# The gated mixture of half 0: summed by TensorE in two PSUM banks and evicted by ScalarE, and the norm of its tiles 0 to 3 applied by ScalarE

## The reference, cut to what matters

```python
x = x + jnp.tanh(g_xattn[0]) * wkv(w, u, _layernorm(x), ctx_2048)      # stage 0 makes y, stage 1 starts from this x
x = x + jnp.tanh(g_ffn[0])   * ternary_ffn(_layernorm(x), w_gate_up, w_proj)
x = x + jnp.tanh(g_xattn[1]) * masked_attention(_layernorm(x), ctx_2048, mask)
x = x + jnp.tanh(g_ffn[1])   * fp8_linear(_layernorm(x), weight, weight_scale, bias)
```

## Time and profile before

| | |
|---|---|
| median of 3 runs | 140.72 us (139.71 to 140.81) |
| the profiled execution | 141.18 us, of which the span from first to last instruction is 139.4 us |
| PE busy | 119.2 us (86% of the span) |
| DVE busy | 116.5 us (84%) |
| ACT busy | 85.5 us (61%) |
| POOL busy | 32.7 us (23%) |
| chain that ended last, by engine | PE 47%, DVE 32%, issue 7%, ACT 6%, DMA 3%, POOL 2% |
| mean granted TensorE clock | 0.951 |

### The profile page before, as it was taken

One profiled execution on the slowest core, in us unless ns is written; L12 is line 12 of the kernel. 1 busy time (PEld: TensorE's weight loads), 2 busy tenths in 40 slices (PEclk: granted clock), 3 DMA queues, 4 the chain that ended last, 5 costly groups with the idle time before them and its releaser, 6 DMA issues.

```text
span 139.4 us, 2211 instructions
## 1 busy us (share of the span) xinstructions
PE 119.2 (86%) x733; PEld 79.6 (57%) x743; DVE 116.5 (84%) x278; ACT 85.5 (61%) x163; POOL 32.7 (23%) x75
## 2 busy tenths in 40 slices
PE   5899788862899899999987999999996779496992
PEld 5799673420522346477653667777675657274581
DVE  5896999997993969999987897769997789995880
ACT  3197898028584777685765777856654534522962
POOL 7913000005000000000233802059334624401000
PEclk9999999995555999999999999999999999999999
DMA  4999950000000000000000000000000000000026
GB/s 132 288 353 350 388 131 2 0 0 0 0 0 0 0 5 2 0 0 0 0 5 0 2 0 0 5 0 0 0 2 5 0 0 0 2 0 0 2 97 208
DMA packets 7110, 6.90 MB, mean 50 GB/s; under 512 B 1336, under 2 KB 6842, under 8 KB 7098
## 3 DMA queue, kind: packets, MB, share of 16 engines
q1 hardware_dynamic: 7088, 6.75, 15.1%
q10 hardware_dynamic: 10, 0.00, 0.0%
HBM read 5.70 MB, written 1.05 MB: 48 GB/s over the span
## 4 chain that ended last, share of the span: by engine, by line
PE 47%; DVE 32%; issue 7%; ACT 6%; DMA 3%; POOL 2%; ACTq 1%; POOLq 0%; DVEq 0%
PE ps L848 8%; PE ps L849 7%; PE ps L907 5%; DVE xs L1214 4%; DVE stats L1125 4%; PE ps L1101 4%; PE ps L881 4%; DVE sums L1156 3%; PE ps L770 3%; PE ps L768 3%; DMA gate_row<-_L_ffn_weight_scale_dram 3%; DVE xn L1137 3%; PE ps L813 2%; PE ps L994 2%; DVE hbuf L1294 2%
## 5 line engine op out<-in xcount | busy, mean ns | idle before, releaser
L848 PE MATMUL ps<-wT,xhi 128*128 128x512 bf16 x60 | 23.8, 396 | 1.3 <-ACT xlo L545 1.0
L849 PE MATMUL ps<-wT,xlo 128*128 128x512 bf16 x60 | 23.5, 392 | 0.2
L907 PE MATMUL ps<-wT,wgu_raw 128*128 128x256 bf16 x128 | 16.6, 273 | 0.1
L418 POOL TENSOR_SCALAR ve<-mv 128x2 f32<-128x2 f32 (+2 forms) x12 | 2.3, 192 | 59.4 <-DVE mv L1131 59.3
L907 PEld LDWEIGHTS ps<-wT,wgu_raw 128*128 128x128 f16 x128 | 12.4, 98 | 1.6 <-DVE wgu_raw L1281 0.3
L1125 DVE BATCH_NORM_STATS2 stats<-xs 128x6 f32<-128x256 f32 x32 | 12.3, 414 | 1.1 <-DMA xs<-in_x_dram 0.7
L586 ACT ACTIVATE wgu_raw<-ps 128x512 f16<-128x512 f32 x16 | 9.6, 597 | 5.5 <-PE ps L881 5.0
L534 ACT ACTIVATE wscale<-ps 128x1024 bf16<-128x1024 f32 x6 | 6.1, 1023 | 10.3 <-PE ps L770 10.3
L1137 DVE TENSOR_SCALAR xn<-xs,mv,rstd 128x256 f32<-128x256 f32 x26 | 9.5, 409 | 2.9 <-POOL rstd L419 2.1
L1294 DVE SCALAR_TENSOR_TENSOR hbuf<-ps,pscale,sil 128x512 f32<-128x512 f32 x11 | 8.2, 749 | 3.3 <-PE ps L849 3.3
L848 PEld LDWEIGHTS ps<-wT,xhi 128*128 128x128 f16 x64 | 6.4, 100 | 7.7 <-ACT xlo L545 1.5
(11 more groups left out here) (173 smaller groups left out, 281.9 us busy)
## 6 DMA issues: line engine op xcount, KB each, us to landing
wgu_raw<-in_L_ffn_w_gate_up_dram SPq DMA_DIRECT2D x4, 512.0 KB, 9.0
ctx_sb<-in_ctx_dram SPq DMA_DIRECT2D x2, 512.0 KB, 7.3
wp_raw<-in_L_ffn_w_proj_dram SPq DMA_DIRECT2D x1, 1024.0 KB, 10.2
out_dram<-xs SPq DMA_DIRECT2D x3, 256.0 KB, 2.2
xs<-in_x_dram SPq DMA_DIRECT2D x2, 256.0 KB, 2.9
xs<-in_x_dram SPq DMA_DIRECT2D x1, 512.0 KB, 6.7
wlin_raw<-in_L_ffn_weight_dram SPq DMA_DIRECT2D x1, 256.0 KB, 9.1
out_dram<-xs SPq DMA_DIRECT2D x2, 128.0 KB, 2.0
```

What stands on the lines that cost most here:

```text
L848: pe.matmul(ps[:, bank, :], xhi[:, h, c, o:o + P], w, start=(c == 0), stop=False)
L849: mm = pe.matmul(ps[:, bank, :], xlo[:, h, c, o:o + P], w, start=False, stop=(c == CH - 1))
L907: mm = pe.matmul(proj_at(i), part[:, n % 2, j * P:(j + 1) * P], wT[:, GU_PAIRS + f, j * C:(j + 1) * C], start=(first and f == 0 and j == 0 ...
```

## The change

TensorE now forms the sum x + tanh(g) * y itself. Two banks are used, 0 for tiles 0 and 1, and 1 for tiles 2 and 3. `mix_x` puts x there, by one float32 matmul of 256 columns per tile against the identity, in the place where the six dummies stood. `mix_y` then accumulates y onto it, in the place of `y_back(0)`: eight float32 matmuls of 128 columns, each with a block of y as the stationary operand and the identity scaled by tanh(g) (`ident_tg`, which ScalarE makes once near the start) as the moving one. ScalarE evicts the two banks to `res` (`mix_in`), ahead of `rest_in(0)`. VectorE's `mix_out` is gone; `mix_stats` is the old `ln_stats` with waits for the evictions. The norm of tiles 2 and 3 moves from VectorE to ScalarE, which now does all four in two steps. `invert(2)` moves on ScalarE from before the norm to behind `xn_low(1)`. `ffn_in(0)` and `ffn_in(1)` wait for one norm step each. `gate(0)` waits for the evictions and the statistics. The rest of the diff adapts counts.

```diff
@@ scalar
             act.preload_act_table_set("natural_log_exp_and_others")
+            act.wait_ge(ident_ready, 1)
+            act.wait_ge(tg_ready, 1)
+            act.activation(ident_tg[:, :], ident[:, :], ACT.Copy, scale=tg[:, 0:1]).then_inc(ident_tg_ready, 1)
             act.wait_ge(cols_ready, 2)
...
+            def mix_in(b):
+                act.wait_ge(mix_ps, b + 1)
+                act.activation(res[:, 2 * b:2 * b + 2, :].rearrange("p i c -> p (i c)"), ps[:, b, :], ACT.Copy).then_inc(mix_ready, 1)
...
             invert(1)
+            mix_in(0)
+            mix_in(1)
             rest_in(0)
             rest_in(1)
-            invert(2)
-            ln_apply(1, 0, TPC // 2, 1)
+            act.wait_ge(mix_ready, 2)
+            ln_apply(1, 0, 2, 1)
+            ln_apply(1, 2, 2, 1)
             xn_high(0)
             xn_high(1)
             xn_low(0)
             xn_low(1)
+            invert(2)
             invert(3)
@@ tensor
+            def mix_x():
+                pe.wait_ge(in_x[0], 16)
+                pe.wait_ge(in_x[1], 16)
+                pe.wait_ge(G_ready, CHUNKS * CH)
+                for i in range(TPC):
+                    o = (i % 2) * C
+                    pe.matmul(ps[:, i // 2, o:o + C], ident[:, :], xs[:, i, :], start=(i % 2 == 0), stop=False,
+                              skip_group_check=True)
+
+            def mix_y():
+                pe.wait_ge(y_ready, CH)
+                pe.wait_ge(ident_tg_ready, 1)
+                for i in range(TPC):
+                    for c in range(CH):
+                        o = (i % 2) * C + c * P
+                        mm = pe.matmul(ps[:, i // 2, o:o + P], y[:, c, i * P:(i + 1) * P], ident_tg[:, :], start=False,
+                                       stop=(i % 2 == 1 and c == CH - 1), skip_group_check=True)
+                    if i % 2:
+                        mm.then_inc(mix_ps, 1)
...
             def ffn_in(k):
...
-                pe.wait_ge(res_ready[1], (1, 1, 2, 3)[k])
-                if k == 0:
-                    pe.wait_ge(xn_ready_act, 1)
+                if k < 2:
+                    pe.wait_ge(ctxT_ready, CHUNKS * CH)
+                    pe.wait_ge(xn_ready_act, k + 1)
...
             def gate(n):
                 if n == 0:
-                    pe.wait_ge(G_ready, CHUNKS * CH)
+                    pe.wait_ge(mix_ready, 2)
+                    pe.wait_ge(mv_ready[1], 1)
...
-            keep_warm(WARM_FRONT, 0, wabs)
+            mix_x()
             for p in range(PAIRS):
                 weight_sums(p)
-            y_back(0)
+            mix_y()
@@ vector
-            def mix_out():
-                dve.wait_ge(tg_ready, 1)
-                dve.wait_ge(yT_ready, 2)
-                residual(1, 0, TPC, lambda i: ps[:, XN_BANKS[0][i // 2], (i % 2) * C:(i % 2 + 1) * C], lambda i: tg[:, 0:1], 1)
+            def mix_stats():
+                last = None
+                for i in range(TPC):
+                    if i % 2 == 0:
+                        dve.wait_ge(mix_ready, i // 2 + 1)
+                    now = step(dve.bn_stats(stats[:, i, :], res[:, i, :]))
+                    if i > 0:
+                        after(last)
+                        step(dve.bn_aggr(mv[:, 1, i - 1, :], stats[:, i - 1, :]))
+                    last = now
+                after(last)
+                dve.bn_aggr(mv[:, 1, TPC - 1, :], stats[:, TPC - 1, :]).then_inc(mv_ready[1], 1)
...
-            mix_out()
-            ln_stats(1, 0, TPC)
+            mix_stats()
             den_bonus(2)
             greatest_scales()
-            ln_apply(1, TPC // 2, TPC // 2, 1)
             den_scan(3)
```

More of the change, by code:

```diff
@@ L100, in gated_blocks @@
         neg_bf = sb("neg_bf", [P, P], BF16)
+        ident_tg = sb("ident_tg", [P, P])
         scales = sb("scales", [SCALE_ROWS, 512], BF16)
@@ L213, in gated_blocks @@
         tg_ready = sem("tg_ready")
+        ident_tg_ready = sem("ident_tg_ready")
+        mix_ps = sem("mix_ps")
+        mix_ready = sem("mix_ready")
         guard_rows = sem("guard_rows")
@@ L787, in y_back @@
                 pe.wait_ge(y_ready, CH * (h + 1))
[L789 to L793, removed]
+                pe.wait_ge(rest_ready, PAIRS)
+                pe.wait_ge(wl_f, 1)
                 for i in range(TPC):
@@ L804, in ffn_in @@
                 bank = XN_BANKS[k // 2][k % 2]
-                pe.wait_ge(res_ready[1], (1, 1, 2, 3)[k])
-                if k == 0:
-                    pe.wait_ge(xn_ready_act, 1)
-                else:
-                    pe.wait_ge(xn_ready[1], k)
+                if k < 2:
+                    pe.wait_ge(ctxT_ready, CHUNKS * CH)
+                    pe.wait_ge(xn_ready_act, k + 1)
+                else:
+                    pe.wait_ge(res_ready[1], k - 1)
+                    pe.wait_ge(xn_ready[1], k - 1)
                 for c in range(CH):
@@ L832, in channel_major @@
                 elif q < 2:
-                    pe.wait_ge(xn_ready_act, q + 2)
+                    pe.wait_ge(xn_ready_act, q + 3)
                 else:
@@ L1218, in residual @@
                 dve.wait_ge(res_ready[stage], count)
-            def mix_out():
-                dve.wait_ge(tg_ready, 1)
-                dve.wait_ge(yT_ready, 2)
-                residual(1, 0, TPC, lambda i: ps[:, XN_BANKS[0][i // 2], (i % 2) * C:(i % 2 + 1) * C], lambda i: tg[:, 0:1], 1)
+            def mix_stats():
[10 more added lines that the diff above has]
+                dve.bn_aggr(mv[:, 1, TPC - 1, :], stats[:, TPC - 1, :]).then_inc(mv_ready[1], 1)
             def mix_pair(k):
-                dve.wait_ge(yT_ready, k + 1)
-                residual(1, 2 * k, 2, lambda i: ps[:, XN_BANKS[1][k - 2], i * C:(i + 1) * C], lambda i: tg[:, 0:1], k)
+                dve.wait_ge(yT_ready, k - 1)
+                residual(1, 2 * k, 2, lambda i: ps[:, XN_BANKS[1][k - 2], i * C:(i + 1) * C], lambda i: tg[:, 0:1], k - 1)
             def weights_abs(p):
@@ L1347, in greatest @@
                 if q < 2:
-                    dve.wait_ge(xn_ready_act, q + 2)
+                    dve.wait_ge(xn_ready_act, q + 3)
                 else:
```

## The result

The changed kernel is slower. Median 142.57 us (141.45 to 144.45, four executions) against 140.22 (139.70 to 140.81) of before, 1.017 times. The ratios given from here on leave disturbed executions out (here that of 144.45 us, in e11 one of 177, whose trace is not read): 1.0127, 95% interval 1.0065 to 1.0190. That is clear of noise, though less than 2%, and the median lies outside the forecast range of 139.0 to 141.7. Timed again in experiment e11 the ratio is 1.0181 (1.0115 to 1.0246). The profiled execution took 141.45, its span is 139.6 us; it is the shortest of its kernel, so its trace shows the least of the loss.

What follows compares the result with a forecast made beforehand. It took the front as bound by VectorE's scan and the scales, then TensorE and ScalarE alternating, then ScalarE alone. Terms -1.05 + 0.55 - 0.1 = -0.6 us, against 140.72 giving 140.1; range 139.0 to 141.7.

Steps and rivals of the forecast that it cites:

- "the same": Whole kernel: no change its measurement can tell, neither under 139.3 us nor over 142.1; chance 0.69.
- The step that failed: GpSimd in the front: statistics 1.6 us sooner, shift at 31.7 instead of 33.31, its 1.2 us of lead unused.
- the front's -1.05: End of the front: ScalarE's norm starts at 32.9 instead of 34.05, so TensorE's turning and `xn_low(1)` come 1.05 us earlier.
- The moved inversion: ScalarE before the table load: a second invert of 1.28 us there gives back 0.55 of the 1.05 us gained.
- The clock: TensorE's clock over `weight_rest(3)`: returning from half earlier than 44.94, it adds 0.1 us of gain, `gate(1)` 0.6 sooner.
- the forecast -0.6: Whole kernel: sum of the terms -1.05, +0.55 and -0.1 us against the profiled execution of before.
- the base: Starting time for the sum: profiled execution 141.18 us, 0.46 above the median; the forecast was set against 140.72.
- `ident_tg` (0.40 us): Start of ScalarE: making the scaled identity takes 0.35 us, hidden in 0.54 us of idle time, so costs 0.
- the evictions: ScalarE ahead of `rest_in(0)`: two at 0.60 us, hidden in 5.45 us of idle time; `rest_in(0)` stays at 29.26.
- the statistics: VectorE in the front: without `mix_out`'s 1.64 us they start at 27.6 instead of 29.20, 1.6 us sooner.
- F: ScalarE behind the table load: an unseen stall up to 0.78 us puts `silu(0)` at 42.6, total 140.9; chance 0.02.
- C: TensorE's clock falls before 27.9 instead of 31.3, slowing `weight_rest(0)` and (1): +0.85 us, 141.6; chance 0.14.

Runs made afterwards that it cites:

- e11: The changed kernel, unedited, timed again beside the kernel before: ratio 1.0181 (1.0115 to 1.0246).
- e2: The changed kernel with one more wait: VectorE starts `den_scan(3)` only once GpSimd has written the shift; ratio to before 1.0017, median 140.35 us.
- e4: The kernel before with only the norm of all four tiles on ScalarE in two steps and `invert(2)` behind `xn_low(1)`; mixture as before; ratio 1.0251.
- e1: The kernel before, unedited, for a second trace: ratio 1.0007, profiled execution 140.55 us.
- e3: The changed kernel with `invert(2)` put back between `rest_in(1)` and the norm: ratio to before 1.0084, median 141.26 us.
- e10: The changed kernel with `quant_here(0)` in the place of `den_scan(3)`, and the scan waiting for the shift: one execution, 140.72 us.
- e9: The changed kernel with VectorE waiting for the shift before `den_bonus(3)`, so only `den_scan(3)` falls beside GpSimd's power: one execution, 140.57 us.
- e6: The changed kernel with `invert(2)` and the norm of two tiles back on their old engines and places, the new mixture kept: ratio to before 1.0032.
- e8: The kernel of e2 with `den_bonus(2)` ahead of `mix_stats` and `invert(2)` between `rest_in(0)` and `rest_in(1)`: ratio to before 0.9959, timed again 0.9989.
- e7: The kernel of e2 with `mix_y` doing one of two channel blocks, so half of y is left out: ratio to before 0.9964.

## Why the prediction was wrong

Forecast 140.1 and "the same" at 0.69; the loss of 1.3% had been given 0.11.

**The step that failed** is "GpSimd starts at 29.45 and the shift is there at 31.7, well before ScalarE is free". It priced GpSimd's three steps at their old durations. But taking `mix_out` and the norm of two tiles from VectorE also moved `den_scan(3)` forward, from behind GpSimd's work to beside it. In the earlier trace rows GpSimd ran from 31.04 to 33.31, while VectorE's list held an idle wait and a one-input norm: the removed `ln_apply` had waited for rstd, and so kept the scan away from the power. The prediction counted this as pure gain ("den_scan, quantizing and the first power of two come earlier by that as well") and asked neither what the removed wait had held back nor what it would run into. Measured: power 2.40 for 1.01, the two small steps 0.56 and 0.52 for 0.20 each, shift 34.04 for the forecast 31.7; worth 1.1 to 1.6% (e2), and 2.4% in e4, there with the clock's second fall.

Term by term, against the first trace of before: the front's -1.05 came out at +0.2 (`xn_low(1)` starts at 38.78 for 38.55). The moved inversion cost 0.4 more (`silu(0)` at 43.05 for 42.40), of 0.55 forecast. The clock gave back 0.4, not 0.1 (`gate(1)` at 45.80 for 45.59). Together +0.2 for the forecast -0.6, and the two profiled times differ by 0.27.

**The third** is the base. The first trace of before had TensorE waiting 0.64 us for the scales; e1's trace is earlier, and there the new matmuls are not hidden. That its best times, 139.4 to 139.7, come from still earlier starts is not shown. Against e1's 140.55 the traced execution of after is 0.9 us longer.

**Right:** `ident_tg` (0.40 us), the evictions and `rest_in(0)` at 29.24 cost nothing; the statistics came 1.3 us earlier; no stall behind the table load (F: 41.76 + 1.28 = 43.04, silu at 43.05); the moved inversion makes ScalarE the last before `silu(0)`; the clock did not fall early (C), and after came back sooner, at 43.1. The moved inversion alone was priced at 0.55 us given back; e3 gives 0.4 to 1.0%, which would be 0.6 to 1.4 us, since the gap before the norm would have hidden it.

**Open.** Why the other executions of after are 1.0 to 1.2 us longer than the traced one, whose span (139.6) is only 0.9 above e1's. A second fall of the clock as in e4 would do it for some: from mean clock and span the time at half clock is an estimated 20 to 21 us in the two of about 144.0 us in e11 (mean clock 0.926 and 0.928), and 10 us in the traced one (0.963). But it is 10 us as well in that of 142.63, and in those of 142.40 and 142.69 in e11 (0.964), which are about 1 us longer all the same. No trace shows where.

## What to carry to other kernels

When an engine is relieved, look at what its removed waits had kept apart: its next instructions move forward, and may land beside a neighbour that they slow. A small GpSimd step on the path wants a VectorE that is idle or at one-input work; one wait on VectorE was worth 1.1 to 1.6% here, and the whole change had been meant to save 0.4%. And count a line's matmuls against the calls in the code before its duration is taken as a price.

## What the runs showed of the hardware

- GpSimd's 128x4 power took 1.01 us alone or beside a reduction, 2.52 beside bf16 two-input operations (e10), and 2.40 beside a float32 scan in every kernel that let the scan meet it (after, e3, e4, e9); VectorE's own durations did not change (scan 1.22 to 1.24).
- Its small steps of 128x4 took 0.19 to 0.24 us beside an idle VectorE or a one-input norm of 128x256 (before, e2, e6, e8, e9), and 0.52 to 0.60 beside two-input operations (after, e4).
- A plain float32 matmul is two matmuls in the record, at full clock 0.13 us each for 128 columns (2.05 for 16) and 0.25 for 256 (1.97 for 8).
- A second half-clock stretch of 3.2 to 3.4 us in the first unit of the loop cost about 1.8 us (e4, e7).
- Near the start, ten dummy transposes took 2.40 us in two traces of before and 1.31 in after's, with a granted clock of 1.00 in the record each time: there the record of the clock and the durations don't agree.
